# Cross-attention: the value matmuls of two steps joined in every second step, with a third buffer of exponentials

## What is computed

```
x = x + self_attention(layernorm(x))
q = layernorm(x) @ Wq.T + bq          # 16 heads of 16, 56 rows
k = ctx @ Wk.T + bk                   # 1500 rows of context for each sequence
v = ctx @ Wv.T + bv
scores = clip(q @ k.T / 4, -50, 50)   # -50 where masked
probs = softmax(scores)
x = x + layernorm(0.05 * ((probs @ v) @ Wo.T + bo)) * gamma + beta
x = x + feed_forward(layernorm(x))
```

## Time and profile before

| | |
|---|---|
| median of 3 runs | 1445.63 us (1444.37 to 1446.39) |
| the profiled execution | 1444.34 us |
| its span, first to last instruction | 1442.4 us |
| PE busy | 1376.7 us, 95% |
| PE weight loads busy | 1176.8 us, 82% |
| DVE, ACT, POOL busy | 70%, 50%, 31% |
| mean granted TensorE clock | 0.98 of full |
| DMA | 46 GB/s on average |

### The profile page before, as it was taken

How to read it: one execution, slowest core, us unless ns; L and a number is a source line. 1 busy time by engine, 2 the same in 40 slices (tenths; PEclk the granted TensorE clock), 3 DMA queues, 4 the chain that set the end, 5 groups by cost and what they waited for, 6 DMA issues and landing times.

```text
span 1442.4 us, 54968 instructions
## 1 busy us (share of the span) xinstructions
PE 1376.7 (95%) x25094; PEld 1176.8 (82%) x25094; DVE 1013.8 (70%) x1792; ACT 716.9 (50%) x939; POOL 447.3 (31%) x400
## 2 busy tenths in 40 slices
PE   5899999998899999999999999999999999999983
PEld 5687787786688888888888888888888888888872
DVE  4676676666136787786777777687878778677765
ACT  3445445444255645555555555555554555555540
POOL 4332333222222333333324233233333333332400
PEclk9999999999899999999999999999999999999995
DMA  9100001000111121111112121111212121121100
GB/s 260 23 1 31 1 1 31 1 30 1 58 49 57 31 77 44 56 58 46 58 37 63 31 77 52 57 49 45 64 31 77 41 62 55 45 61 34 49 2 7
DMA packets 38808, 66.75 MB, mean 46 GB/s; under 512 B 3605, under 2 KB 36818, under 8 KB 38578
## 3 DMA queue, kind: packets, MB, share of 16 engines
q1 hardware_dynamic: 38578, 63.24, 15.1%
HBM read 61.40 MB, written 1.84 MB: 44 GB/s over the span
## 4 chain that ended last, share of the span: by engine, by line
PE 71%; DVE 2%; issue 0%; POOL 0%; POOLq 0%; DVEq 0%
PE proj_ps L1277 19%; PE proj_ps L1268 19%; PE score_ps L1295 14%; PE sum_ps L1315 12%; PE side_ps L1350 2%; PE side_ps L1332 2%; PE side_ps L1364 1%; PE side_ps L1357 1%; PE side_ps L1339 0%; DVE inv L1109 0%; DVE exps L1097 0%; DVE amax L1150 0%; DVE hidden L1182 0%; DVE hidden L1193 0%; DVE sig L1192 0%
## 5 line engine op out<-in xcount | busy, mean ns | idle before, releaser
L1049 ACT ACTIVATE exps<-score_ps 125x1792 f32<-125x1792 f32 x192 | 320.5, 1669 | 419.0 <-PE score_ps L1295 419.0
L1097 DVE TENSOR_SCALAR exps<-exps,top 125x896 f32<-125x896 f32 x384 | 287.9, 791 | 18.0 <-ACT exps L1049 17.5
L1295 PE MATMUL score_ps<-spread,keys 32*125 32x112 f32 x6144 | 219.3, 279 | 0.0
L1315 PEld LDWEIGHTS sum_ps<-exps,vals 125*32 125x32 f32 x12288 | 163.0, 110 | 50.9 <-issue 34.4
L1088 DVE COPY vals<-proj_ps 125x512 f32<-125x512 f32 x192 | 128.2, 687 | 103.4 <-PE proj_ps L1277 103.0
L1295 PEld LDWEIGHTS score_ps<-spread,keys 32*125 32x125 f32 x6144 | 185.1, 183 | 15.4 <-issue 0.4
L1315 PE MATMUL sum_ps<-exps,vals 125*32 125x56 f32 x12288 | 191.5, 214 | 2.9 <-DVE exps L1097 2.9
L992 POOL TENSOR_TENSOR low<-raw_early,high 128x500 fp32r<-128x500 f32 x64 | 100.8, 1583 | 231.2 <-issue 115.4
L992 POOL TENSOR_TENSOR low_early<-raw_early,high_early 128x500 fp32r<-128x500 f32 x62 | 104.3, 1691 | 172.3 <-issue 104.1
L1041 ACT ACTIVATE keys<-proj_ps,b_k 128x500 f32<-128x500 f32 x192 | 129.9, 677 | 52.4 <-PE proj_ps L1268 52.4
L286 POOL TENSOR_TENSOR swapped<-swapped,sin 128x448 f32<-128x448 f32 (+1 forms) x72 | 88.6, 1232 | 138.5 <-ACT swapped L507 138.5
(11 more groups left out here) (156 smaller groups left out, 2411.6 us busy)
## 6 DMA issues: line engine op xcount, KB each, us to landing
raw_early<-in_ctxT SPq DMA_DIRECT2D x64, 500.0 KB, 4.0
raw<-in_ctxT SPq DMA_DIRECT2D x32, 500.0 KB, 3.5
w_q<-in_attn_Wq SPq DMA_DIRECT2D x4, 512.0 KB, 8.1
w_o<-in_attn_Wo SPq DMA_DIRECT2D x1, 2048.0 KB, 21.5
out<-y_out SPq DMA_DIRECT2D x16, 112.0 KB, 1.9
rows<-in_x SPq DMA_DIRECT2D x1, 1344.0 KB, 16.8
raw_early<-in_ffn_gate_wT SPq DMA_DIRECT2D x1, 1024.0 KB, 9.6
raw_early<-in_ffn_val_wT SPq DMA_DIRECT2D x1, 1024.0 KB, 5.1
```

Of the source, the lines that this page charges most:

```text
L1049: nc.scalar.activation(exps[t % 2][:, :, :, :].rearrange("p h r n -> p r h n"), score_ps[0:TILE, :, 0:2 * QW].rearrange("p r (h n) -> p r ...
L1097: nc.vector.tensor_scalar(tile, tile, LIMIT_LO, top[:, n, at:at + 1], ALU.max, ALU.min)\
L1295: ins = nc.tensor.matmul(score_ps[0:TILE, r, to:to + HE * S], keys[c % 2][32 * r:32 * r + 32, k, (at + half) * TILE:(at + half + 1) * TILE ...
L1315: ins = nc.tensor.matmul(sum_ps[32 * h:32 * h + VW, g, :], vals[c % 2][:, at + half, HJ * g + h, :], exps[t % 2][:, half, r, col:col + S], ...
```

## The change

In every odd step `add_up` is left out; in every even step it is called twice, for t-2 and t-1 (at t = 0 for the last two steps of the pair before). The exponentials therefore live one step longer and get a third buffer, and `exp_twin` waits for the `add_up` of step t-3, which used its buffer last. At the last pair's last step the `add_up` of step 10 is called by itself, as it was before. The number of matmuls, their operands' shapes and all other engines' work stay the same. A constant is added that nothing uses.

```
-        exps = [sb(f"exps{n}", [TILE, 2, HR, QW]) for n in range(2)]
+        exps = [sb(f"exps{n}", [TILE, 2, HR, QW]) for n in range(3)]
...
                 if warm:
-                    act.wait_ge(probs_used, NT * i + t - 1)
-                nc.scalar.activation(exps[t % 2][:, :, :, :].rearrange("p h r n -> p r h n"),
+                    act.wait_ge(probs_used, NT * i + t - 2)
+                nc.scalar.activation(exps[t % 3][:, :, :, :].rearrange("p h r n -> p r h n"),
...
-                    exp_twin(i, t, not first or t >= 2)
+                    exp_twin(i, t, not first or t >= 3)
...
-                tile = exps[t % 2][:, half, :, :].rearrange("p r n -> p (r n)")
+                tile = exps[t % 3][:, half, :, :].rearrange("p r n -> p (r n)")
...
-                                exps[t % 2][:, half, r, col:col + S],
+                                exps[t % 3][:, half, r, col:col + S],
...
-                    if t:
-                        add_up(i, t - 1, not first or t - 1 >= BN)
-                    elif not first:
-                        add_up(i - 1, NT - 1, True)
+                    for back in (2, 1) if t % 2 == 0 else ():
+                        if t:
+                            add_up(i, t - back, not first or t - back >= BN)
+                        elif not first:
+                            add_up(i - 1, NT - back, True)
+                    if last and t == NT - 1:
+                        add_up(i, NT - 2, True)
```

More of the change, by code:

```diff
@@ L48 @@
 N_EARLY = 11 + 2 * HJ
+WEIGHTS_AT = 13
 TILE = 125
```

## The result

| | |
|---|---|
| before, median of 6 runs beside the changed kernel | 1445.19 us (1442.31 to 1449.57) |
| after, median of 6 runs | 1455.88 us (1454.70 to 1458.41) |
| ratio, 95% interval | 1.0074 [1.0055, 1.0092] |
| the profiled execution after, its span | 1454.70 us, 1452.9 us |

The kernel is slower by some 10.7 us, where +0.6 was forecast: outside the range, beyond its upper end of 1452. In the changed kernel all later lines move by one: scores L1296, keys L1269, values L1278, `add_up` L1316, `project` L1333, limit L1098, the products L1114 and L1115.

What follows compares the result with a forecast made beforehand. PE was taken to bound the kernel, never waiting in the steady state. Joins at -12.7 us and waits at `project` at +13.3 us gave +0.6 us, a median of 1446.2 us, range 1432 to 1452.

Steps and rivals of the forecast that it cites:

- The join: Two value blocks back to back on PE save one turn between matmul kinds: 94 x 0.135 = -12.7 us.
- The buffer: Third buffer of exponentials and looser wait of `exp_twin`: adds no wait, costs nothing.
- Values into scores: V (value projection) now runs into scores instead of `add_up`: 0.33 us against 0.32, so nothing comes back.
- the turn: PE's switch to another kind of matmul around each `add_up` block: 0.14 us.
- The wait at `project`: At t = 2 PE would wait for DVE's `heads`, 0.95 us in pairs 2 to 15: +13.3 us.
- The wake-up: PE's delay in starting `project` after `heads` are ready: 0.09 us, between nothing and 0.18.
- The products are held by GpSimd: Earlier GpSimd operations block DVE's products L1113 and L1114 in the first divide: 1.2 to 1.3 us each instead of 0.39.
- Rival A: DVE's products are not held by GpSimd, so `heads` arrive in time: 1433.5 us, chance 0.22.
- B: Port alternation costs DVE one more meeting of 0.4 us between two divides per pair: 1452 us, chance 0.13.
- rival C's second half: PE's queue runs short within 128 narrow matmuls; with the no-gain alternative, 1459 us or more, joint chance 0.06.
- The sum itself: PE's joins, -12.7 us, plus waits at `project`, +13.3 us: net +0.6 us, median 1446.2 us.
- the pace of 12.3 ns: Start-to-start spacing of the 64 value matmuls in an `add_up` block, taken as evidence against PE's queue running short.

Runs made afterwards that it cites:

- the keys' run: Joined kernel with the early divide, even steps reordered to scores, first piece of keys, both value blocks, second piece of keys; 1475.23 us, ratio 1.0212.
- the early divide: Changed kernel with DVE's divide of a pair's first sequence moved from step 0 of the next pair to step 7 of its own; 1446.08 us.
- the one with 589 increments: Joined kernel with the early divide plus 589 empty PE semaphore increments, at most 12 ahead of a joined block, steering packet boundaries away; 1454.51 us.

## Why the prediction was wrong

**Right, with sizes.** The join: 1.71 us from a joined block's start to the scores, forecast 2 x 0.925 - 0.135 = 1.715; pairs without a stop or wait are 0.84 us shorter, forecast 0.81. The buffer: nothing, as forecast and as its own run shows. Values into scores did not pay the turn back: otherwise the 0.84 would not be there. The wait at `project`: 0.88 us, forecast 0.95, but full in 11 pairs and not in 14, since stops cover three, and 0.65 us in the first pair, where none was forecast; the list has 13.0 us in 13 waits over the whole run, forecast some 17 in 15. The wake-up took 0.06 us instead of 0.09 (646.56 to 646.62), the rest of the difference was not followed.

**Right, with its reason.** The products are held by GpSimd: 1.24 and 1.32 us, forecast 1.25 each; the limits behind them are free again (1.51 us for two, forecast 1.6). Rival A is out, and so is B: no further meeting came. The Trainium skill, "SBUF — State Buffer", on the shared port pair, gave this result by its rule for two SBUF inputs, and the trace agrees with it, 1.24 against 0.39 us.

**Wrong: rival C's second half, "PE's queue runs short within 128 narrow matmuls"**, at a chance of 0.06, priced together with a join that gains nothing (1459 us or more). The sum itself puts the supply of PE's instructions at nothing. The reason that I gave against it was the pace of 12.3 ns over one block of 64. That pace does hold in 128. But what runs short is not inside a block: it is the supply of instructions over the block and the scores together, and a row of one block, or of a kernel whose longest dense stretch is 192 instructions, cannot show what 320 do. The missing term is the stops: 14.2 us in the 14 pairs, against nothing in the forecast. The joins there came to -11.8 us against -11.3, the waits to 9.7 against 13.3: 14.2 - 0.5 - 3.6 = 10.1, which is what the measured +10.7 lies above the forecast +0.6. Had no stop covered a wait, joins and waits would have come to -11.8 + 12.3 = +0.5 there, against +2.0: without the stops the forecast would have held, by this sum. I had asked of every engine and buffer whether it would be late, but not of PE's own instruction queue, which stands on the page.

**What stays open.** Why a packet is sometimes asked for 1.3 to 3.3 us after the matmuls reach a boundary, where 0.6 to 1.2 is usual, was not settled; the longest stops and those of the keys' run are of this kind. Executions of one kernel differ by 4 to 14 us, and the longer ones mostly have the lower mean granted clock: the kernel before took 1441.0 to 1444.2 us at 0.982 or more and 1444.2 to 1447.2 at 0.979 or less, the one with the early divide 1439.3 to 1442.1 at 0.982 or more and 1445.1 to 1448.9 at 0.980 or less, the one with 589 increments 1449.40 at 0.981 and 1463.07 at 0.973. In the profiled executions of the kernel before, the changed one and the one with the early divide the clock is 1.00 from 385 to 1395 us. Where in the others it fell, and whether a stop came first each time, as in the one case above, no trace shows.

## What to carry to other kernels

Before PE's work is packed more densely, count how many instructions will follow without a wide matmul among them, and look at where the program's packets of instructions end: PE can run out of instructions while every engine and buffer is in time, and an idle stretch put down to "issue" in the middle of one block is the sign. Such a stop depends on the place in the program, so an edit elsewhere can switch it on or off; compare an order with a version that leaves the instruction count alone, and use the denser order only where it fits. And a gain on the engine that bounds needs the margin of each of its waits: here one of 0.24 us turned into a wait as large as the gain, and moving work that was ready earlier (the divide) took it away at no cost.

## What the runs showed of the hardware

- PE's instructions arrive in packets of 16.4 KB, some 256 instructions. In all stops of the stage, in every kernel here that has any, PE restarts at such a boundary, 1.2 to 1.7 us after a packet has landed that itself took 0.9 to 1.4 us.
- A packet starts only about when the one before it comes into use: in the changed kernel 0.6 to 2.0 us after the matmuls reach a boundary 44 to 150 instructions behind the start of a joined block, and up to 2.5 us ahead of them where it lies within the first 42, just behind wide matmuls.
- A stop has 0.2 to 2.9 us of idle time, listed as "issue"; by starts it costs more (1.45 us where the list has 1.19).
- The granted clock can fall behind a stop: 0.51 from 638.8 to 642.3 us behind one of 1.23 us, wide matmuls then at half the pace.
- An empty semaphore increment on PE costs some 0.14 us where nothing hides it (64 of them, 8.9 us) and nothing measurable between matmuls in the single order (443 of them, pairs unchanged), but in the joined order many of them ahead of a dense block made the stops worse.
- 128 value matmuls start at the same pace as 64: (1.78 - 0.21) us over 128, 12.3 ns.
